# GpSimd issues a token gather five tiles ahead of ScalarE's gate, in place of nine gathers at once

## What is computed

```python
x = x + 0.5 * _L0_ffn_ref(_layernorm(x), router_w, router_b, w1, w2)
x = x + _L0_attn_ref(_layernorm(x), ...)
x = x + 0.5 * _L0_ffn_ref(_layernorm(x), router_w, router_b, w1, w2)

# _L0_ffn_ref: 8 experts, each token goes to the one with the highest logit
logits = x @ router_w + router_b
route = softmax(logits); max_prob = max(route); max_ind = argmax(route)
for e in range(8):
    a, g = split(x @ w1[e])              # 128 -> 512 and 512
    y = silu(a) * g @ w2[e]              # 512 -> 128
    out = where(max_ind == e, y, out)
out = out * max_prob
```

## Time and profile before

| | |
|---|---|
| timed runs, median | 426.67 us |
| span of the profiled execution | 421.5 us |
| first expert loop, first transpose to end of last scatter | 28.95 to 103.64 us |
| second expert loop, the same | 344.10 to 417.43 us |
| TensorE busy over the span | 373.5 us (89%) |
| gathers, median on GpSimd | 0.97 us each, 46 of them |

### The profile page before, as it was taken

How to read it: one execution, slowest core, us unless ns; L and a number is a source line. 1 busy time by engine, 2 the same in 40 slices (tenths; PEclk the granted TensorE clock), 3 DMA queues, 4 the chain that set the end, 5 groups by cost and what they waited for, 6 DMA issues and landing times.

```text
span 421.5 us, 8456 instructions
## 1 busy us (share of the span) xinstructions
PE 373.5 (89%) x2962; PEld 339.5 (81%) x2962; DVE 309.6 (73%) x475; ACT 261.8 (62%) x508; POOL 260.0 (62%) x190
## 2 busy tenths in 40 slices
PE   7398999996799988999999899999998298999994
PEld 7297988896664377899998789999898297998994
DVE  2844454472699699999999999999979845544561
ACT  2314333341397999999999999999645414433330
POOL 7054666654001009999999999999960054666643
PEclk9679999999699999999999999999999689999999
DMA  6928592210300168654444344434337321121110
GB/s 197 346 61 253 131 406 64 47 33 32 101 0 4 30 165 20 150 158 132 126 158 155 125 126 166 144 130 130 108 117 285 90 40 41 38 47 46 40 39 25
DMA packets 42730, 47.47 MB, mean 113 GB/s; under 512 B 13313, under 2 KB 34370, under 8 KB 42178
## 3 DMA queue, kind: packets, MB, share of 16 engines
q1 hardware_dynamic: 37634, 39.72, 31.7%
q0 software_dynamic: 2944, 6.13, 6.1%
q10 hardware_dynamic: 2112, 1.08, 1.2%
HBM read 37.38 MB, written 9.54 MB: 111 GB/s over the span
## 4 chain that ended last, share of the span: by engine, by line
ACT 35%; PE 16%; DVE 15%; POOL 3%; issue 2%; another core or an unknown queue 1%; DMA 1%; POOLq 0%; DVEq 0%; ACTq 0%
ACT phase L1050 16%; ACT phase L1060 14%; PE psum L660 9%; PE psum L672 5%; DVE xc L1287 4%; DVE phase L966 3%; POOL w_sb L885 2%; DVE x_tok L1012 1%; ACT dt L920 1%; DVE xc L1283 1%; PE psum L1151 1%; PE psum L1183 1%; POOL phase L373 1%; DMA phase<-token_rows,token_row 1%
## 5 line engine op out<-in xcount | busy, mean ns | idle before, releaser
L885 POOL TENSOR_TENSOR w_sb<-phase,w_sb 128x1024 f32<-128x1024 f32 x62 | 144.7, 2378 | 0.0
L966 DVE TENSOR_TENSOR_SCAN phase<-phase,psum 128x1024 f32<-128x1024 f32 x64 | 142.1, 2272 | 3.0 <-PE psum L1133 2.3
L660 PE MATMUL psum<-phase 128*128 128x128 f32 x736 | 92.1, 277 | 4.6 <-ACT phase L559 2.9
L660 PEld LDWEIGHTS psum<-phase 128*128 128x128 f32 x736 | 86.5, 192 | 6.8 <-ACT phase L559 3.5
L373 POOL DMA_INDIRECT phase<-token_rows,token_row x46 | 47.2, 1027 | 55.3 <-DVE token_row L475 25.8
L1050 ACT ACTIVATE phase<-dtxT,B_cols 128x256 f32<-128x256 f32 x192 | 79.9, 495 | 0.2
L1151 PE MATMUL psum<-ident,w_sb 128*128 128x128 f32 x512 | 67.5, 276 | 3.3 <-DVE silu_z L959 0.9
L1060 ACT ACTIVATE phase<-dt,neg_A 128x1024 f32<-128x1024 f32 x64 | 69.6, 1136 | 0.0
L496 DVE TENSOR_TENSOR phase<-phase,psum 128x512 f32<-128x512 f32 x46 | 31.4, 684 | 45.1 <-PE psum L660 21.8
L1151 PEld LDWEIGHTS psum<-ident,w_sb 128*128 128x128 f32 x512 | 56.5, 141 | 8.7 <-POOL w_sb L885 6.9
L1124 PE MATMUL psum<-ident,phase 128*128 128x128 f32 x384 | 55.6, 276 | 1.5 <-DVE phase L966 0.6
(11 more groups left out here) (180 smaller groups left out, 401.5 us busy)
## 6 DMA issues: line engine op xcount, KB each, us to landing
w_sb<-c_rows SPq DMA_DIRECT2D x32, 512.0 KB, 3.9
w_sb<-ffn_w SPq DMA_DIRECT2D x16, 512.0 KB, 7.3
B_diag<-dt SPq DMA_DIRECT2D x4, 1024.0 KB
phase<-B_diag SPq DMA_DIRECT2D x32, 128.0 KB, 3.8
w_sb<-ffn_w SPq DMA_DIRECT2D x8, 256.0 KB, 7.8
token_rows<-x_tok SPq DMA_DIRECT2D x4, 264.0 KB, 4.9
token_rows<-x_tok ACTq DMA_DIRECT2D x4, 264.0 KB, 6.0
x_tok<-attn_x SPq DMA_DIRECT2D x4, 256.0 KB, 4.1
```

The source lines that it names most:

```text
L660: last = nc.tensor.matmul(psum[:, 2 * k + part, c * P:(c + 1) * P], w1_tile[:, t % W1_RING, part * F + c * P:part * F + (c + 1) * P], xsT_ ...
L885: nc.gpsimd.tensor_tensor(hC[:, k % HC_RING, :], H[:, k % H_RING, :], C_sb[:, j % C_RING, :], ALU.mult).then_inc(M["hC_ready"], 1)
L966: nc.vector.tensor_tensor_scan(H[:, k % H_RING, :], dA[:, k % DECAY_RING, :], dBx_bank[k % SLOTS], 0.0, ALU.mult, ALU.add).then_inc(M["sca ...
```

## The change

Four gathers are issued without a wait. Gather 4 waits until ScalarE has copied the transposes of tiles 0 and 1. From gather 5 on, gather t waits until `gate_ready` has reached t-4, that is until silu(t-5) is done. Scatter t now stands two turns of the loop later in GpSimd's program, behind gather t+7.

```diff
-    XS_RING, AHEAD, YS_RING = 10, 8, 4
+    XS_RING, AT_ONCE, YS_RING = 10, 4, 4
...
                 if t >= XS_RING:
                     pool.wait_ge(f["ys_ready"], t - XS_RING + 1)
+                if t == AT_ONCE:
+                    pool.wait_ge(f["xsT_ready"], 2)
+                elif t > AT_ONCE:
+                    pool.wait_ge(f["gate_ready"], t - AT_ONCE)
                 nc.gpsimd.indirect_dma_start(xs_sb[:, t % XS_RING, :], None, token_rows,
...
-            for t in range(AHEAD):
+            for t in range(AT_ONCE + 1):
                 gather(t)
             for t in range(SLOT_TILES):
-                if t + AHEAD < SLOT_TILES:
-                    gather(t + AHEAD)
+                if t + AT_ONCE + 1 < SLOT_TILES:
+                    gather(t + AT_ONCE + 1)
+                if t >= LAG:
+                    scatter(t - LAG)
+            for t in range(SLOT_TILES - LAG, SLOT_TILES):
                 scatter(t)
```

## The result

Ten timed runs of the changed kernel have a median of 428.94 us (426.44 to 431.62), ten of the kernel before, on the same chip, 425.20 us (423.92 to 427.33). The ratio is 1.0076, with a 95% interval of 1.0045 to 1.0106: the change costs 1.9 to 4.5 us. The forecast of 429.6 us holds.

The account below looks back on a forecast made before the run. TensorE was taken to bound both expert loops, at 2.79 us a tile. Late gathers 2.9 us, scatters 0 and burst 0, added to the median of 426.67, gave 429.6 us; range 420.5 to 432.5 us.

Parts of the forecast that it names:

- The gathers are late in both busy stretches of the first loop: First loop, 34 to 42 and 50 to 63 us: paced gathers land late, 2.2 to 3.6 us, taken as 2.9; chance 0.40.
- The scatters move: GpSimd's queue: each scatter loses at most the 1.25 us gather ahead, covered by the ring of four result slots; 0.
- The burst is gone: Both loops: starts give back 2.6 us, gathers passing later cost 2.2; taken as 0, bounds +2.2 to -8 us.
- the holds: Both loops: TensorE's signals reach ScalarE late, perhaps held by GpSimd's run of nine gathers; idle 2.52 and 3.38 us.
- The second loop loses nothing by lateness: Second loop: gathers land in 2.81 us, need 3.8 us with norm and silu, have 5.58 us; no loss.
- The sign: Second loop, profile after: no wait for a DMA after gather 4 would show the forecast right.
- Cancels or is hidden: Rival: late gathers never reach TensorE or cancel with the burst's gain; -2 to +2 us, about 426.5 us; chance 0.30.
- The holds end: Rival, both loops: gathers paced by ScalarE no longer hold TensorE's signals; 6 to 10 us back, 417 to 424 us; chance 0.30.
- Lookahead too short everywhere: Rival: paced gathers above 4.6 us in the second loop too, both loops at gather latency; no chance of its own.

Follow-up runs that it names:

- kernel before with late clears: The kernel before, with the 4 MB of clears of B_diag issued behind the first expert loop: 429.29 us, ratio 1.0086.

## Why the prediction came out right, step by step

- **The gathers are late in both busy stretches of the first loop: right as a mechanism, with the size too small.** The term was 2.2 to 3.6 us, of which I took 2.9. The first loop paced alone costs 5.3 to 8.4 us, and on the chip where nothing is held the whole change costs 5.9 to 9.6 us. In the profile after, the first stretch adds 2.65 us to the first loop (forecast 1.0 to 1.5, or 0 to 0.4 against the trace) and the second 2.92 (forecast 1.2 to 2.1). Three things were missing in the chain.
  - *Gather 4.* I had gather 6 go out at 35.9, after the silu(1) of the trace before. But silu(1) stands behind norm(4), and gather 4, issued just as the weights begin to pass, now takes 5.91 us (3.97 before, from 30.95 to the norm at 34.92). Gather 6 went out at 37.46. Gather 5 was nearly as forecast: issued at 32.59 (33.3), silu(2) at 40.35 (40.7 to 41.2).
  - *The clock.* "The granted clock is 1.00 in both, so the clock plays no part" was true of before only. After the wait in the first stretch, hidden(3) costs 3.02 us in place of 1.95 and down(0) 1.76 in place of 1.06: 1.8 us. hidden(4) started at 43.14, not at 41.5 to 42.0, in a loop whose first transpose came 1.1 us earlier (27.82, not 28.95). In the second stretch of this profile the clock stayed full.
  - *The scatter ahead.* "The gate that this gather waits for is always there first" looked at the scatter behind the gather, not at the one in front of it. silu(6) ended at 51.71 (51.12 + 0.59), but gather 11 had to wait for scatter 3, itself late behind gather 10, and went out at 54.15: 2.44 us later. From silu(6) to norm(11) there are 10.43 us, where I had reckoned 7.06 to 7.49.
- **The scatters move: 0, right, but wrongly described.** They do not move behind two more gathers. The first scatter stood behind nine gathers and stands behind eight, so in GpSimd's program each scatter is one gather earlier. In time it comes later where the gather ahead of it waits, as scatter 3 does behind gather 10. Where nothing is held, the second loop is 70.93 us after and 70.74 before, moved scatters and all.
- **The burst is gone: I took 0; the slower chip gives something back.** The second loop alone is 0.5 to 2.8 us faster, within the bounds of -8 to +2.2 us. The idle at its start is gone as forecast, and the excess comes back beyond tile 7. In the profiles of the slower chips the three paced second loops take 75.75 to 77.07 us, the three unpaced ones 76.89 to 81.75, against 70.7 to 72.1 on the faster. So pacing takes away about a quarter of the holds there: 1.7 us (by the ratio) of the 6.15 by which the second loop before is longer on the slower chip. The same change costs 5.9 to 9.6 us without holds and 1.9 to 4.5 us with them, and these intervals do not meet. The second loop explains 1.7 us of that. In the first loop the two causes may overlap: a gather that is late while a signal is held anyway would cost nothing more. This is argued and not shown, since the first loop paced alone lost 5.3 to 8.4 us on a slower chip, nearly as much as the change without holds.
- **The second loop loses nothing by lateness: right in sum.** I had written that no wait for a DMA follows gather 4 there. There are such waits, 2.33 us at 361.90 among them. On the faster chip the change has waits of up to 2.35 us in this loop after the one for gather 0, and 21 of its 22 steps between transposes are at 2.79 us or below: TensorE's pace does not feel them. The sign was ill chosen: a wait on ScalarE is no loss until a transpose is late.
- **The rivals.** "Cancels or is hidden" is half true: a part cancels, too little to come to nothing. "The holds end" has its mechanism in part, but the paced stream holds signals too, as was argued against it. "Lookahead too short everywhere" is out. The figure that the Trainium skill gives in "DMA: Bandwidth & Descriptors", section "Anatomy of one DMA" (the estimate was 2.2 us a gather, and no loss) is near what lightly used DMA engines show (2.6 to 4.3 us from issue to norm where ScalarE waits in the second loop after, and 2.81 in the earlier trace rows). It is too low by about a factor of three beside 2.25 MB of weights or 4 MB of clears (5.8 to 8.0 us in the profile after).
- **The base.** The forecast added 2.9 us to the three runs' 426.67. The kernel before measured 425.20 beside the change, so the measured difference is 3.7 us by medians, 3.2 by the ratio.

By the middle of the ratios, late gathers cost 7.8 us where nothing is held, and the change costs 3.2 us where signals are. Of the 4.6 us between them the second loop gives back 1.7, and the cause of the other 2.9 is open. The forecast had 2.9 for the late gathers and 0 for the burst.

## What to carry to other kernels

How far ahead a prefetch must run is set by the latency in the worst stretch that it crosses, 7 to 8 us here, and not by the mean or by the idle 3 us: five tiles of 2.79 us less the work and the queue between were too few, and eight were enough on the faster chips, the only ones where they were tried. When a load is made to wait for a consumer, follow the chain a full turn round (load, norm, gate, next load, with every scatter in between), since each delay issues the next load later. The old order was at times hardly further ahead, but a late load there did not delay the ones behind it. Add the clock to the upper bound of any new wait on TensorE, also where the clock is full before the change.

## What the runs showed of the hardware

**The same kernel takes 425 us on one chip and 412 us on another, and the difference lies in its gather loops.** The kernel before has loops of 78.63 and 76.89 us in the first profile and of 71.95 and 70.74 us in the last: 12.83 us together. The part between the loops takes 236.90 and 237.95 us. The medians differ by 12.6 us (425.20 and 412.58), so the holds are no matter of profiling. In these two profiles, on the faster chip 21 and 22 of the 22 steps between transposes in the two loops are at the pace of 2.79 us or below. On the slower one 13 and 16 are, and the others take 2.95 to 4.52 us. The start of the second loop shows one such place. The timeline of ScalarE for the kernel before on the faster chip: norm(4), silu(1) and the copy of tile 3.

```profile
342.77 0.50 ACT L551 ACTIVATE phase<-phase 128x128 f32<-128x128 f32 x1
343.17 0.59 ACT L565 ACTIVATE phase<-psum 128x512 f32<-128x512 f32 x1
343.64 0.27 ACT L559 COPY phase<-psum 128x128 f32<-128x128 f32 x1
```

The copy follows at once, where it followed an idle 3.38 us in the first profile, with the same nine gathers before it. In the kernel before with late clears, on the slower chip, TensorE even loses its clock by such an idle at the start of the second loop: hidden(2) takes 2.93 us, at a granted clock of 0.66, after 2.34 us of nothing.

```profile
357.48 2.93 PE L660 MATMUL psum<-phase 128*128 128x128 f32 x16 [2.34 <-issue]
...
360.20 0.42 PE L648 MATMUL psum<-ident,phase 128*128 128x128 f32 x1
```

What the chips differ in, and whether and through what GpSimd's stream delays TensorE's signals, is not settled. It was seen only that the excess lies where gathers are issued: in the last part of each loop, where only scatters are left, and between the loops the two kinds of chip keep the same pace. The run that leaves gathers out fell on a faster chip, so that the gathers themselves are the cause was not tested.

**A wait of TensorE can cost more than its length.** In the profile after, down(0) and hidden(3) cost 1.8 us more than at the full clock. With the first loop alone paced four groups do, 3.4 us in all: down(0) takes 2.07 us (the granted clock is 0.50 there, the lower level of 1.2 GHz in place of 2.4) and hidden(3) 2.58, then down(6) 1.76 and hidden(9) 3.02. In the long profile of the change on the faster chip it is 4.0 us: hidden(3) in 3.27 us, down(6) in 2.07 and hidden(9) in 3.62. But the waits before down(6) and hidden(9) in the profile after cost no clock. So the price is a bound and not a sum that can be foretold from the length of the wait.
